# Layer 0's experts of a two-layer net: computed for every token, or by expert order with fetched rows and weights

## The chip, the cores and the metric

The kernel runs on one core of a Trainium2 chip (trn2). The metric is device time in microseconds (us) of one execution, smaller is better; three executions of the kernel before gave 1397.77, 1398.66 and 1400.67 us. Engines are named as the profile names them: PE (TensorE, matmuls; PEld is its weight load), DVE (VectorE), ACT (ScalarE), POOL (GpSimd), SP (SyncE, here only a DMA queue). DMA transfers are issued by SP, or by POOL where the rows to be fetched come from a table of indices.

## The reference, cut to what matters

The input is 2 sequences of 512 tokens, 256 wide: 1024 tokens. Two layers, each `x + s * silu(ffn)`, where `s` is attention and both parts read the same normalised rows:

```python
xn = _layernorm(x)
s = attn0(xn)                       # causal softmax attention, 16 heads of 16
g = silu(ffn0(xn)); x = x + s * g
xn = _layernorm(x)
s = attn1(xn)                       # gated delta rule, 16 key heads of 128, 32 value heads
g = silu(ffn1(xn)); x = x + s * g   # 2 shared and 16 routed experts, top 2

def ffn0(x, router_w, w1, w2, w3):  # 8 experts, 256 -> 128 -> 256
    logits = xf @ router_w.T
    topk_vals, topk_idx = jax.lax.top_k(logits, 2)
    topk_weights = softmax(topk_vals)
    gate = silu(einsum('nd,edf->enf', xf, w1))
    value = einsum('nd,edf->enf', xf, w2)
    expert_out = einsum('enf,efd->end', gate * value, w3)
    return sum over the two chosen of expert_out * topk_weights
```

The reference computes all 8 experts for every token and then selects two. Only 2048 of the 8192 (token, expert) pairs count.

## The kernel before, in words

Tokens lie in 8 tiles of 128 (n = 0 to 7; sequence b has tiles 4b to 4b+3). The program is one list. `Plan` holds pieces of work, each with parts on engines, a cost for each part and what it comes after. `Plan.arrange` (L128) repeatedly takes the ready piece that could start earliest by those costs, in steps of `GRAIN`, with ties decided by rank plus the engine's offset in the table `RANK`. What comes out is one order for each engine, which every engine then follows strictly, and the PSUM banks (8 of 128 x 2 KB) of each piece. So a piece that waits holds up all that stands behind it on its engine. The costs only make the order.

Layer 0 in the order of its work:

- The prologue loads inputs (among them the expert weights w1, w2, w3, 3 MB), normalises, makes Q, K, V. Q and K are written to DRAM and read back by 24 DMAs of 256 KB in another layout (`stack`).
- `rt`, `tp`: router logits, the two best of 8, their softmax, and by `gates` a table `gate` of 8 weights a token (six of them zero).
- Experts, dense: 16 blocks (expert e, sequence b). `exg` and `exv` are together 4 matmuls of 512 columns (L977), the two `exd` pieces 4 of 256 (L985). The profile counts each fp32 matmul of the code twice, so a block is 8 of L977 and 8 of L985 there. ACT takes silu (L1857), DVE the product (L1509) and the weighted sum into `facc` (L1521, L1523).
- Softmax: 64 pieces `p1` (scores on PE L995 and L1000, row maxima on DVE L1531), 32 for each sequence. When 32 are done `tn` (L1008, L1549) turns the maxima, SP writes them out and reads them back (`max`), and from then on the 16 steps of that sequence run: `sc` scores (L1016), exp on ACT (L1872), causal mask on POOL (L2097), `pv` (L1026). After each four steps `ov` (L1037) and a DVE reciprocal (L1555) and POOL product `am` (L2102).
- `op` (L1045): the output projection, on DVE `+bo` (L1560), times silu(experts) (L1562), plus x (L1564). `nrm`, `nr2`: the second layernorm. `ln1`: transposes into XH and XL.

Layer 1 begins with `gt` (router and gates, L930, at b = 0 and 1), convolution pieces `ck`, `cq`, `cv` (PE L930, DVE L1644: three operations a tile), up projections, then a chain of 64 units (`M` L1715 is its first DVE piece; L930 at 342.84 us stands in it), in whose gaps the remaining work is put. Layer 1's routed experts already work on rows in expert order: `cnt` counts and `places` computes tables (DVE L1405 to L1458), `slot` turns them to row numbers; for each group of 4 tiles of 128 rows `sr` fetches token rows (POOL L2135), `sw` weight rows (POOL L2151), `sT` transposes (PE L1169), `su` is the up product (PE L1178), `sd` down; `ss` (SP) writes the result rows, and `cb` fetches, for each token, its two result rows (POOL).

Of the kernel before, what the change touches and what calls it, by code (L numbers as in the profile page):

```python
# [30 lines left out]
GROUPS = (TILES + 3) // 4  # L31


def constants():
# [21 lines left out]


# [17 lines left out]
    "fWK": {"POOL": -59.896, "SP": -107.701}, "fWO": {"POOL": -20.631, "SP": 61.337},
    "fWV": {"POOL": 38.893, "SP": -91.558}, "fin": {"DVE": 5.828, "SP": -47.444}, "fs": {"ACT": 9.746},
    "fup": {"POOL": 27.276, "SP": -11.99}, "g0": {"ACT": -40.647}, "gg": {"DVE": -120.429, "PE": -10.129},
    "gram": {"DVE": 32.752, "PE": -0.939}, "gt": {"ACT": -141.264, "PE": -153.565},
    "kn": {"ACT": -7.778, "PE": -1.885, "POOL": -40.681}, "kns": {"ACT": 1.445},
    "ln1": {"ACT": -114.142, "DVE": -74.072, "PE": -25.594}, "max": {"SP": -146.911}, "mk": {"POOL": -21.707},  # L80
# [2220 lines left out]
```

## Time and profile before

| | us |
|---|---|
| median of 3 | 1398.66 (1397.77 to 1400.67) |
| profiled execution, its own time | 1398.75 |
| its span on the core | 1397.0 |
| PE busy | 1332.1 (95%) |
| DVE busy | 1127.7 (81%) |
| ACT busy | 950.0 (68%) |
| POOL busy | 698.5 (50%) |

The profile page gives busy time by engine, and in "slices" the share of 40 equal stretches. From the third slice on, PE is at 8 or 9 tenths to the end. The chain that ended last is 63% PE, 20% DVE, 6% ACT. The granted TensorE clock (PEclk, 1.0 is 2.4 GHz) is at 7 to 9 tenths in parts of the first seven slices and 9 later. Of the chain 4% is PE L977 and 2% PE L985, the dense experts. DMA is nearly full in the first two and a half slices (loads and the `stack` reads) and at some 2 tenths afterwards.

### The profile page before, as it was taken

What the parts mean: (1) busy time and instruction counts of PE and PEld (TensorE: products, weight loads), DVE (VectorE), ACT (ScalarE), POOL (GpSimd) and SP (SyncE); (2) the same over time, 40 slices, a digit from 0 to 9 for tenths busy, and PEclk for the clock granted to TensorE, in tenths of its full rate; (3) what the DMA queues carried; (4) which work ended last, traced back from release to release, by engine and by line L of the source; (5) the groups of instructions that cost most, each with busy time, mean ns of one, the idle gap of its engine ahead of it and who ended that gap; (6) DMA issues with size and microseconds to landing.
All of it is one profiled execution on the core that took longest, in us unless ns stands there. A gap on an engine that the chain in (4) does not pass through costs nothing.

```text
span 1397.0 us, 32580 instructions
## 1 busy us (share of the span) xinstructions
PE 1332.1 (95%) x12308; PEld 1089.2 (78%) x12308; DVE 1127.7 (81%) x2294; ACT 950.0 (68%) x2607; POOL 698.5 (50%) x806
## 2 busy tenths in 40 slices
PE   6999999788999999999999999999999998999997
PEld 3544446566888888888988898989888987889896
DVE  4487436889978788879798879797978888979886
ACT  3105752376777768787878787777777776787784
POOL 8012222328745475474655555656646558546431
PEclk9979999889999999999999999999999999999999
DMA  9950001212211121121311311312212114111000
GB/s 323 125 76 1 4 1 45 76 34 70 49 28 31 35 89 34 37 83 41 82 42 32 88 36 38 86 31 80 49 26 80 32 44 113 37 27 32 24 2 31
DMA packets 59507, 76.68 MB, mean 55 GB/s; under 512 B 6200, under 2 KB 46776, under 8 KB 59352
## 3 DMA queue, kind: packets, MB, share of 16 engines
q1 hardware_dynamic: 54616, 60.31, 17.9%
q0 software_dynamic: 4736, 14.29, 3.7%
q8 instruction: 98, 1.61, 0.5%
q14 instruction: 57, 0.47, 0.1%
HBM read 62.92 MB, written 11.67 MB: 53 GB/s over the span
## 4 chain that ended last, share of the span: by engine, by line
PE 63%; DVE 20%; ACT 6%; issue 4%; DMA 3%; POOL 3%; SPq 0%; POOLq 0%; DVEq 0%; ACTq 0%
PE ps L930 11%; PE ps L1313 6%; DVE yv L1644 4%; PE ps L977 4%; PE ps L1266 3%; DMA RC<-crow 3%; PE ps L1295 3%; PE ps L1282 2%; DVE yk L1644 2%; PE ps L1228 2%; PE ps L1218 2%; PE ps L1231 2%; PE ps L1267 2%; PE ps L985 2%; PE ps L1291 2%
## 5 line engine op out<-in xcount | busy, mean ns | idle before, releaser
L1988 ACT ACTIVATE XY<-ps 128x512 f16<-128x512 f32 x384 | 221.2, 599 | 71.4 <-PE ps L1231 70.2
L1734 DVE TENSOR_TENSOR ZL<-ps,cst 128x256 f16<-128x256 f32 x384 | 154.8, 418 | 34.7 <-PE ps L1218 34.0
L1644 DVE SCALAR_TENSOR_TENSOR yv<-ps,cw,yv 128x511 f32<-128x511 f32 (+2 forms) x192 | 143.4, 747 | 7.0 <-ACT yv L1925 2.3
L930 PE MATMUL ps<-XH,WVh 128*128 128x256 f32 (+1 forms) x384 | 133.4, 347 | 1.3 <-ACT hT L1973 1.3
L1313 PE MATMUL ps<-WO,OGT 128*128 128x256 f32 x512 | 126.3, 390 | 2.4 <-DVE OGT L1806 2.2
L930 PE MATMUL ps<-XH,WVl 128*128 128x256 f32 (+1 forms) x384 | 123.0, 320 | 0.0
L930 PE MATMUL ps<-XL,WVh 128*128 128x256 f32 (+1 forms) x384 | 122.8, 320 | 0.0
L2181 POOL TENSOR_TENSOR RC<-RC,dec 128x512 f32<-128x512 f32 x64 | 69.2, 1081 | 99.1 <-DMA RC<-crow 99.0
L1228 PE MATMUL ps<-ZL,XY 128*128 128x64 f16 x1536 | 105.5, 193 | 4.1 <-DVE ZL L1734 3.2
L2021 ACT ACTIVATE sq<-O 128x128 bf16<-128x128 f32 x256 | 79.8, 312 | 38.5 <-DVE O L1793 16.1
L1231 PE MATMUL ps<-XY,ZL 128*128 128x64 f16 x1536 | 105.0, 193 | 0.0
L1218 PEld LDWEIGHTS ps<-XY,LT 128*128 128x128 f16 x1536 | 80.2, 98 | 31.6 <-issue 12.4
L1218 PE MATMUL ps<-XY,LT 128*128 128x64 f16 x1536 | 100.5, 193 | 3.8 <-ACT XY L1988 2.4
L1313 PEld LDWEIGHTS ps<-WO,OGT 128*128 128x128 f32 x512 | 92.8, 191 | 13.5 <-issue 1.6
L1228 PEld LDWEIGHTS ps<-ZL,XY 128*128 128x128 f16 x1536 | 78.7, 97 | 29.1 <-issue 13.5
L2027 ACT ACTIVATE O<-O,small 128x128 f32<-128x128 f32 x256 | 82.7, 411 | 12.5 <-POOL small L2212 12.4
L1295 PEld LDWEIGHTS ps<-De,PT 128*128 128x128 f32 x512 | 74.4, 191 | 8.1 <-ACT De L2012 1.8
L1295 PE MATMUL ps<-De,PT 128*128 128x128 f32 x512 | 78.3, 278 | 1.7 <-ACT De L2012 1.6
L930 PEld LDWEIGHTS ps<-XH,WVl 128*128 128x128 f32 x384 | 72.5, 189 | 5.7
L2202 POOL TENSOR_TENSOR XY<-LT,cst 128x512 f16<-128x512 f16 x64 | 74.8, 1169 | 4.0 <-DVE W L1755 1.1
L930 PEld LDWEIGHTS ps<-XH,WVh 128*128 128x128 f32 x384 | 72.7, 189 | 4.7 <-ACT hT L1973 1.5
L2210 POOL TENSOR_SCALAR small<-small 128x4 f32<-128x4 f32 x64 | 12.5, 195 | 126.2 <-ACT sq L2021 123.8
(305 smaller groups left out, 4126.6 us busy)
## 6 DMA issues: line engine op xcount, KB each, us to landing
RC<-crow SPq DMA_DIRECT2D x128, 128.0 KB, 4.0
WV<-in_WV SPq DMA_DIRECT2D x16, 512.0 KB, 3.6
WK<-in_WK SPq DMA_DIRECT2D x16, 256.0 KB, 2.8
WO<-in_WO SPq DMA_DIRECT2D x16, 256.0 KB, 2.7
rows_out<-st SPq DMA_DIRECT2D x7, 512.0 KB, 4.3
KS<-spread SPq DMA_DIRECT2D x12, 256.0 KB, 19.3
QS<-spread SPq DMA_DIRECT2D x12, 256.0 KB, 26.8
w<-in_w SPq DMA_DIRECT2D x4, 512.0 KB, 8.6
```

The lines of the kernel that those rows point to most:

```text
L930: m = pe.matmul(o, a, b, start=c + k == 0, stop=c == 1 and k == 2)
L1218: m = pe.matmul(ps[:, bk, 64 * l:64 * l + 64], LT[:, u % 3, l, :], half(xy(u, 0)[:, l, :], k, 0), start=True, stop=True)
L1228: pe.matmul(ps[:, bk, 64 * l:64 * l + 64], y, half(z, k, 0), start=True, stop=True)
L1231: m = pe.matmul(ps[:, bk, 256 + 64 * l:320 + 64 * l], z, half(y, k, 1), start=True, stop=True)
L1295: m = pe.matmul(ps[:, bk, 256 + 128 * v:384 + 128 * v], PT[:, u % 4, 2 * b + v, :], De[:, b, v, :], start=True, stop=True)
L1313: m = pe.matmul(ps[:, bk, 256 * b:256 * b + 256], OGT[:, 2 * b + v, :], WO[:, h % 2, v, :], start=v == 0, stop=v == 1)
L1644: m = dve.scalar_tensor_tensor(out=dst[:, k:512], in0=ps[:, bk, 0:512 - k], scalar=cw[:, h, j, 3 - k:4 - k], in1=dst[:, k:512], op0=ALU.mu ...
L1734: leave(dve.tensor_tensor(half(ZL[:, k - 2], k, 0), p, lv(k), ALU.mult), "a", u, k)
L1988: leave(act.activation(changed(u, k), ps[:, bank("b", u, k), :].rearrange("p (c n t) -> p c n t", c=2, t=1 << (k - 1)), ACT.Copy), "b", u, k)
L2021: act.activation(sq[:, 1, :], O[:, u % 2, l, :], ACT.Square, accum_out=so[:, u % 2, l:l + 1]).then_inc(s_sqo, 1)
L2027: m = act.activation(O[:, u % 2, l, :], O[:, u % 2, l, :], ACT.Copy, scale=ro[:, u % 2, l:l + 1])
L2202: pool.tensor_tensor(xy(u, 1), LT[:, u % 3], spread4(cst[:, C_Y1:C_Y1 + 128]), ALU.mult).then_inc(s_y1, 1)
```

## The change

The dense experts of layer 0 are replaced by routed ones, of the same design as layer 1's. 1024 tokens with 2 experts each are 2048 rows; sorted by expert and padded to 128 for each of 8 experts they fill at most 16 + 7 = 23 tiles, in 6 groups of four (the last has three).

```diff
+TILES0 = 2 * 1024 // 128 + 7
+GROUPS0 = (TILES0 + 3) // 4
...
-    for k in range(16):
-        e, b = divmod(k, 2)
-        rank = -100 + 2 * k
-        old = [(("exd", *divmod(k - 3, 2), q), "PE") for q in range(2)] if k > 2 else []
-        x, y = ("exg", e, b), ("exv", e, b)
...
+    P.add(("xr0",), -400, ("SP", 1.0))
+    P.add(("cnt0",), -500, ("PE", 3.5, (("tp", 2), "DVE")), ("DVE", 9.0), takes=True, gives=("cnt0",))
+    P.add(("slot0",), -500, ("PE", 1.2, (("cnt0",), "DVE")), ("DVE", 0.2), takes=True, gives=("slot0",))
+    for g in range(GROUPS0):
+        rank = -400 + 6 * g
+        tiles = range(4 * g, 4 * g + tiles_of(g, TILES0))
+        old = [(("sd0", g - 2, q), "PE") for q in range(2)] if g > 1 else []
+        for t in tiles:
+            P.add(("sw0", t), rank, ("POOL", 1.0, (("cnt0",), "DVE"), (("sd0", g - 2, t % 4 // 2), "PE") if g > 1 else (("xr0",), "SP")), ("DMA", 1.9))
+            P.add(("sr0", t), rank, ("POOL", 1.0, (("slot0",), "DVE"), (("sT0", g - 1), "PE") if g else None), ("DMA", 0.8))
+        P.add(("sT0", g), rank, ("PE", 0.88, *[(("sr0", t), "DMA") for t in tiles]),
+              ("ACT", 0.91, (("sv0", g - 1), "PE") if g else None), takes=2, gives=("sT0", g))
+        P.add(("sg0", g), rank + 1, ("PE", 1.85, (("sT0", g), "ACT"), *[(("sw0", t), "DMA") for t in tiles]),
+              ("ACT", 0.62, *old), takes=True, gives=("sg0", g))
+        P.add(("sv0", g), rank + 2, ("PE", 1.85, (("sg0", g), "PE")), ("DVE", 0.6, (("sg0", g), "ACT")), takes=True, gives=("sv0", g))
         for q in range(2):
+            P.add(("sd0", g, q), rank + 3, ("PE", 0.92, (("sv0", g), "DVE")), ("DVE", 0.6, (("ss0", g - 1), "DMA") if g else None), takes=True, gives=("sd0", g, q))
+        P.add(("ss0", g), rank + 3, ("SP", 0.4, (("sd0", g, 0), "DVE"), (("sd0", g, 1), "DVE")), ("DMA", 2.6))
+    for n in range(NT):
+        P.add(("cb0", n), -400 + n, ("POOL", 2.2, (("ss0", GROUPS0 - 1), "DMA"), (("cb0", n - 4), "DVE") if n > 3 else None),
+              ("DMA", 0.8), ("DVE", 0.8))
     for b in range(2):
-        P.add(("g0", b), -60, ("ACT", 1.7, *[(("exd", 7, b, q), "DVE") for q in range(2)], (("g0", 0), "ACT") if b else None))
+        P.add(("g0", b), -200, ("ACT", 1.7, *[(("cb0", n), "DVE") for n in range(4 * b, 4 * b + 4)]))
...
+                elif x[0] == "sr0":
...
+                    pool.indirect_dma_start(rows0[:, k, :], None, xn0d, bass.IndirectOffsetOnAxis(ap=toki[:, t:t + 1], axis=0)
+                                            ).then_inc(d_in0[k], 16)
+                elif x[0] == "sw0":
...
+                    pool.indirect_dma_start(weights0[g % 2][k], None, A["ud0"],
+                                            bass.IndirectOffsetOnAxis(ap=rowi[:, t:t + 1], axis=0)).then_inc(d_wt0[g % 2][k], 16)
+                elif x[0] == "cb0":
+                    n = x[1]
+                    w.wait_ge(d_res0, 16 * GROUPS0)
...
+                    for k in range(2):
+                        pool.indirect_dma_start(wt0[:, n % 4, 256 * k:256 * k + 256], None, rows_out0,
+                                                bass.IndirectOffsetOnAxis(ap=posi[:, k, n:n + 1], axis=0)).then_inc(d_cb0[n % 4], 16)
```

`xr0` writes the normalised rows to DRAM (1 MB, `xn0d`). `cnt0`, `slot0` and `places` make the tables (`rowi`: weight rows of a tile; `toki`: token of each row; `posi`: where each token's two results lie). A group then takes 8 gathers on POOL (`sw0` 384 KB each, `sr0` 128 KB each), 8 transposes and an ACT copy (`sT0`), 8 matmuls of 128 columns for each of `sg0` and `sv0`, 4 of 256 for `sd0`, two DVE copies and one write of 512 KB (`ss0`). The weights have two sets of four buffers, the rows one: `sr0` of a group waits for the transposes of the group before. After the last group's write has landed, `cb0` makes 16 gathers, two for each n, and two DVE operations each; `g0` (silu) and `om` need them. The weights w1, w2, w3 are no longer loaded in the prologue; the host hands them over as one table `ud0` of rows of 3 KB.

Further parts: `op` is split. `op` (PE and DVE `+bo`) is free of the experts, `om` holds the two DVE operations that need them. `ln1` no longer comes after all expert matmuls. All of `RANK` has other numbers, for instance

```diff
-    "p1": {"DVE": 26.78, "PE": -1.261}, "pl": {"POOL": -95.917}, "pre": {"ACT": -110.761, "DVE": -90.125},
+    "p1": {"DVE": 25.623, "PE": -1.244}, "pl": {"POOL": -69.883}, "pre": {"ACT": -134.502, "DVE": -91.138},
-    GRAIN = 0.09700
+    GRAIN = 0.03900
-    DELAY = {"PE": 0.22, "DVE": 0.18, "ACT": 0.24, "POOL": 0.19, "SP": 0.1, "DMA": 0.1}
+    DELAY = {"PE": 0.22, "DVE": 0.18, "ACT": 0.24, "POOL": 0.19, "SP": 0.1, "DMA": 2.0}
```

and in layer 1 the planned DMA cost of `sr`, `sw`, `cb` is 0.8 in place of 2.5, and the write `ss` counts 0.4 on SP and 2.6 as DMA in place of 4.5 on SP. So the order of layer 1 changes too.

What stands on POOL around the begin of the softmax. The names: L2068 and L2070 split layer 1's first weights, L2097 is the mask, L2102 is `am`; before:

```order
L2068 CAST WKh<-WK 128x512
L2070 TENSOR_TENSOR WKl<-WK,WKh 128x512
L2068 CAST wabh<-wab 128x160
L2070 TENSOR_TENSOR wabl<-wab,wabh 128x160
L2097 AFFINE_SELECT PT<-PT 128x4x128 x8
L2102 TENSOR_TENSOR aT<-OT,rB 128x512
```

In the changed kernel the same place (L2127 is the split, L2202 `sw0`, L2190 `sr0`, L2154 the mask):

```order
L2127 TENSOR_TENSOR wabl<-wab,wabh 128x160
L2202 DMA wt<-in_ud,rowi 128x768 x4
L2190 DMA rows<-xn0d,toki 128x256 x4
L2202 DMA st<-in_ud,rowi 128x768 x2
L2202 DMA wt<-in_ud,rowi 128x768 x2
L2190 DMA rows<-xn0d,toki 128x256 x4
L2202 DMA wt<-in_ud,rowi 128x768 x4
L2190 DMA rows<-xn0d,toki 128x256 x4
```

So the first gathers stand behind the split of the weights, and the gathers of groups 0 to 3 ahead of the first mask. Further down POOL has the write-backs' gathers `cb0` (L2213) between two groups of masks, 13 masks ahead of them:

```order
L2154 AFFINE_SELECT PT<-PT 128x4x128 x3
L2159 TENSOR_TENSOR aT<-OT,rB 128x512
L2154 AFFINE_SELECT PT<-PT 128x4x128 x3
L2213 DMA wt<-rows_out,posi 128x256 x16
L2154 AFFINE_SELECT PT<-PT 128x4x128 x3
```

All 16 gathers stand together; the 14th to 32nd masks are behind them.

On PE, the rows ahead of the turned maxima of sequence 0 (L1008 before). Before, dense expert matmuls stand between the `p1` pieces:

```order
L985 MATMUL ps<-w,hT 128x256 x4
L995 MATMUL ps<-KS,QS 128x128 x2
L1000 MATMUL ps<-cb 128x128 x2
L995 MATMUL ps<-KS,QS 128x256 x2
L1000 MATMUL ps<-cb 128x128 x2
L977 MATMUL ps<-xnT,w 128x512 x2
```

In the changed kernel (L1041 and L1046 are `p1`, L1013 `sT0` of group 1, L1023 `sg0` and `sv0`, L1054 `tn`):

```order
L1013 MATMUL ps<-cst,rows 128x128 x8
L1041 MATMUL ps<-KS,QS 128x384 x2
L1046 MATMUL ps<-cb 128x128 x2
L1041 MATMUL ps<-KS,QS 128x512 x2
L1046 MATMUL ps<-cb 128x128 x2
L1041 MATMUL ps<-KS,QS 128x128 x2
L1046 MATMUL ps<-cb 128x128 x2
L1023 MATMUL ps<-XS,st 128x128 x4
L1023 MATMUL ps<-XS,wt 128x128 x4
L1041 MATMUL ps<-KS,QS 128x256 x2
L1046 MATMUL ps<-cb 128x128 x2
L1054 MATMUL ps<-cst,Mp 32x128 x4
```

So `tn` of sequence 0 now stands behind `sT0`, `sg0` and `sv0` of group 1 (`sv0` repeats the two L1023 rows right ahead of L1054). In the changed kernel 42 `p1` pieces and the matmuls of two groups stand ahead of the first `sc`; before, 44 `p1` pieces 20 of the 64 matmuls of L977 and 12 of the 64 of L985. Ahead of the first `M` of layer 1, the changed order has more of layer 1's other PE work than before (K convolution 60 matmuls for 42, V 36 for 12, Z 36 for 24, up 12 for 24), and seven more convolution tiles on DVE.

## Rows read from the trace of the kernel before

**Rows 1.** Windows view: stretches of the span by engine, granted clock, DMA share.
```profile
core 0: us, PE busy (x) PEld busy (x) DVE busy (x) ACT busy (x) POOL busy (x), PEclk, DMA share, GB/s
65.00:104.00 39.00, 38.28 (x194) 19.19 (x192) 34.93 (x53) 1.88 (x2) 4.49 (x6) 0.74 0.63 83
104.00:212.00 108.00, 106.57 (x616) 49.00 (x614) 57.09 (x67) 66.11 (x89) 29.16 (x39) 1.00 0.01 2
212.00:258.00 46.00, 36.68 (x135) 23.66 (x134) 34.39 (x82) 8.61 (x18) 13.83 (x16) 0.92 0.17 55
258.00:320.00 62.00, 51.79 (x256) 42.93 (x257) 53.50 (x127) 40.10 (x85) 20.67 (x24) 0.86 0.18 52
320.00:1397.00 1077.00, 1044.79 (x10949) 925.15 (x10948) 920.51 (x1882) 816.09 (x2386) 601.77 (x710) 0.99 0.19 49
```

**Rows 2.** Chain that ended last, in time: start us, us, what; dense matmuls, `cnt`, layer 1.
```profile
228.14 1.73 PE ps L985 x8
229.87 3.43 PE ps L977 x8
296.61 3.41 PE ps L1153 x16
342.84 1.49 PE ps L930 x6
```

**Rows 3.** PE timeline (start us, us, engine, line, operation): routed group of layer 1.
```profile
490.29 1.56 PE L1178 MATMUL ps<-st,wt 128*128 128x128 f32 x12
```

**Rows 4.** POOL timeline around the end of the stack reads.
```profile
87.31 0.61 POOL L2068 CAST WKh<-WK 128x512 fp32r<-128x512 f32 x1 [57.99 <-DMA WK<-in_WK]
91.52 0.52 POOL L2070 TENSOR_TENSOR wabl<-wab,wabh 128x160 fp32r<-128x160 f32 x1
```

**Rows 5.** POOL timeline: two row gathers of layer 1, one after the other.
```profile
341.42 0.95 POOL L2135 DMA_INDIRECT st<-xnd,toki  x1 [0.30 <-issue]
342.67 0.95 POOL L2135 DMA_INDIRECT st<-xnd,toki  x1 [0.30 <-issue]
```

**Rows 6.** DMA issues of the whole span: KB each where known, median us to landing.
```profile
st<-xnd,toki POOLq DMA_INDIRECT x31, 3.6
wt<-in_ud,rowi POOLq DMA_INDIRECT x24, 4.5
rows_out<-st SPq DMA_DIRECT2D x7, 512.0 KB, 4.3
```

**Rows 7.** One line's landings (L2135, the row gathers), with their spread.
```profile
DMA to landing us min/median/max: 2.7/3.6/5.1
```

**Rows 8.** PE timeline: `tn` of sequence 0, then the first score.
```profile
97.07 0.60 PE L1008 MATMUL ps<-cst,Mp 128*32 128x128 f32 x4
104.02 0.51 PE L1016 MATMUL ps<-QS,KS 64*128 64x512 f32 x2
```

**Rows 9.** Windows view of one PE line each: L1016 (`sc`), then L1026 (`pv`).
```profile
104.00:212.50 108.50, 26.50 (x128) 11.94 (x128) 1.00 0.01 2
...
104.00:212.50 108.50, 23.86 (x256) 5.03 (x256) 1.00 0.01 2
```

**Rows 10.** PE timeline, end of layer 0: last `pv`, last `op`, first gates.
```profile
212.03 0.42 PE L1026 MATMUL ps<-PT,V 128*32 128x128 f32 x8
241.76 5.34 PE L1045 MATMUL ps<-wo,aT 128*128 128x256 f32 x24
258.29 0.69 PE L930 MATMUL ps<-XH,wabh 128*80 128x512 f32 x1 [3.75 <-DVE XL L1585]
```

**Rows 11.** Groups by shape, 0 to 330 us: busy us, mean ns, idle; the reciprocal.
```profile
L1555 DVE RECIPROCAL rB<-ps 128x512 f32<-128x512 f32 x8 | 26.9, 3358 | 11.0 <-PE ps L1037 11.0
```

**Rows 12.** DVE timeline: a convolution tile; layer 1's first `M`; an `op`.
```profile
264.54 2.31 DVE L1644 SCALAR_TENSOR_TENSOR yk<-ps,cw,yk 128x511 f32<-128x511 f32 x3
320.31 0.68 DVE L1715 TENSOR_TENSOR M<-ps,E 128x512 f32<-128x512 f32 x1
253.56 0.42 DVE L1560 TENSOR_TENSOR st<-ps,bo 128x256 f32<-128x256 f32 x1
```

More of the change, by code:

```diff
@@ L75 @@
[L75 to L80, printed above, removed]
@@ L91 @@
-    "su": {"ACT": -16.946, "PE": 8.309}, "sw": {"DMA": -100.52, "POOL": -124.214}, "sx": {"POOL": -65.71},
-    "tn": {"DVE": -40.39, "PE": -186.124}, "tn0": {"DVE": -59.954}, "top": {"ACT": -153.89, "DVE": -156.062},
[3 rows of a table removed]
[4 rows of a table added]
+    "cb": {"DMA": 53.563, "DVE": 100.046, "POOL": 124.422}, "cb0": {"DMA": -7.938, "DVE": 19.605, "POOL": 12.029},
+    "cc": {"POOL": 17.016}, "ck": {"ACT": -22.284, "DVE": 80.478, "PE": -3.081}, "cnt": {"DVE": 1.226, "PE": -22.434},
+    "cnt0": {"DVE": -18.804, "PE": -2.993}, "cq": {"ACT": -46.76, "DVE": 50.605, "PE": -1.71},
@@ L96 @@
+    "sv0": {"DVE": 45.357, "PE": 6.262}, "sw": {"DMA": -51.94, "POOL": -99.591}, "sw0": {"DMA": 6.433, "POOL": 1.813},
+    "sx": {"POOL": -65.71}, "tn": {"DVE": -93.687, "PE": -200.173}, "tn0": {"DVE": -40.719},
+    "top": {"ACT": -195.908, "DVE": -148.291}, "tp": {"ACT": 69.034, "DVE": -62.104},
[3 rows of a table added]
 }
@@ L987, in run_tensor @@
+                    signal(m, *x)
+                elif what == "sd0":
+                    g, q = x[1:]
+                    bk = enter(*x)
+                    w.wait_ge(*done("sv0", g))
+                    for k in range(2 * q, min(2 * q + 2, tiles_of(g, TILES0))):
+                        m = pe.matmul(ps[:, bk, 256 * (k % 2):256 * (k % 2) + 256], hT0[:, g % 2, 128 * k:128 * k + 128],
+                                      weights0[g % 2][k][:, 512:768], start=True, stop=True)
                     signal(m, *x)
@@ L1502, in run_vector @@
                     softmax_of_two()
-                    gates(0, 8, 7)
-                elif what == "exv":
-                    e, b = x[1:]
-                    h_ = hT0[:, (2 * e + b) % 3, :]
-                    w.wait_ge(*done("exg", e, b))
+                    choose(0, 8)
+                elif what == "cnt0":
+                    places(("cnt0",), 0, 8)
+                elif what == "slot0":
+                    w.wait_ge(*full("slot0"))
+                    leave(dve.tensor_copy(toki[:], ps[:, bank("slot0"), 0:32]), "slot0")
+                elif what == "sv0":
+                    n = 128 * tiles_of(x[1], TILES0)
+                    w.wait_ge(*done("sg0", x[1]))
@@ L1558, in run_vector @@
                     w.wait_ge(*full(*x))
+                    for q in range(2):
+                        w.wait_ge(*full("sd0", GROUPS0 - 1, q))
+                    leave(dve.tensor_tensor(st[:, n, :], ps[:, bank(*x), 0:D], bo[:], ALU.add), *x)
+                elif what == "om":
+                    n = x[1]
+                    w.wait_ge(*done("op", n))
                     w.wait_ge(s_g0, n + 1)
-                    leave(dve.tensor_tensor(st[:, n, :], ps[:, bank(*x), 0:D], bo[:], ALU.add), *x)
-                    w.wait_ge(*done(*x))
                     dve.tensor_tensor(st[:, n, :], facc[:, n, :], st[:, n, :], ALU.mult).then_inc(s_og, 1)
```

407 lines of the change are left out of this document (225 added, 182 removed), and 24 rows, old and new, of the table RANK.

## The prediction, made before the changed kernel ran

> **What bounds the kernel now.** I read the windows first: they show who is busy in each stage. In all of layer 1 from 320 us on, PE is busy 1044.8 of 1077 us; in the softmax stage 104 to 212 us it is 106.6 of 108, at full clock [rows 1]. So up to 247 us, the end of the last output projection [rows 10], PE work taken away would count in full if nothing else came in. From 258 to 320 us the table of the first row turns: DVE is busy 53.5 of 62 us and PE waits for it [rows 1]. The chain in time shows the dense experts as links of 3.43 us (eight matmuls of L977) and 1.73 us (eight of L985), one behind the other [rows 2]. Ahead of 104 us the POOL timeline and the PE timeline say why the softmax doesn't start sooner: layer 1's first weights land at 87.3 us behind the stack reads, the queue's end [rows 4], and `tn` stands at 97.07, the first score at 104.02 [rows 8].
>
> **PE work.** Removed: 16 blocks x (3.43 + 1.73) = 82.6 us [rows 2]. Added: layer 1's routed group shows 12 matmuls of 128 columns in 1.56 us, 0.13 each [rows 3]; the profile counts each of the code twice, so `sg0` and `sv0` are 16 each, 4.2 us; eight transposes of that width 1.0; `sd0` has the shape of a block's L985, 1.7. That is 6.9 us a group of four and 39.7 for 5.75 groups. `cnt0` and `slot0` are as in layer 1, where 16 matmuls of `cnt` took 3.41 us [rows 2]; there are twice as many with its other half, at most 6.8, and fp16 ones in `slot0`: between 4 and 9, I take 7. Net: 82.6 - 39.7 - 7 = 36 us less on PE. If PE stayed as full as it is, the kernel would take 1363.
>
> **What it adds: a chain of transfers.** Two gathers in a row start 1.25 us apart on POOL [rows 5] and land 3.6 us after issue [rows 6]; weight rows 4.5. On POOL, `sw0` and `sr0` stand behind the split of layer 1's weights, over at 92.0 [rows 4]; the tables they need are ready long before by my reading (the count runs while the stack is read), so the in-order queue is what makes them late, not their data. Four `sw0`, four `sr0`: the last is issued at 92.0 + 8 x 1.25 - 1.25 = 100.8 and lands at 104.4. Only then can `sT0` of group 0 run, and PE, in order, stands there with 22 of 64 `p1` done. Before, PE had 38.3 of 39 us filled here [rows 1]. Group 1's eight are issued by 110.8 and land at 114.4. Behind that on PE: transposes 1.0, copy on ACT 1, `sg0` 2.0, a `p1`, `sv0` 2.0, and with the clock at the level of 0.74 that rows 1 show here, some 1.2 us more: `tn` at 121.6 or later, in place of 97.07. From `tn` to the first score 6.95 us go by for the round trip of the maxima [rows 8]: 128.6. PE work that piles up at low clock could make it 134. I take **131, 27 us later**.
>
> **From the first score to the end of the projections.** Before: 104.0 to 247.1 (241.76 + 5.34), 143 us [rows 8, 10], some 2 of it idle. 44 of 64 of the 977 and 52 of 64 of the 985 matmuls lie in it: 54.9 x 44/64 + 27.7 x 52/64 = 60.2. So the rest is 81 us: softmax, `p1`, `op`. After: 131 + 81 + 1.5 (two more `p1`) + 3.75 groups x 6.9 = 25.9, makes 239 if PE never waits. It does, at two places.
>
> First, groups 2 to 5 wait for gathers again: `sr0` of a group stands behind transposes of the group before and behind masks, and each costs at least one landing, 3.6 us [rows 6], that softmax pieces cover in part. Between 0 (all covered) and 4 x 5.1 = 20 (the slowest landing of rows 7, none covered) I take 8.
>
> Second, the write back. `sd0` of group 5 stands on PE behind 13 further `p1`, 23 of 64 score pairs, 8 of 32 `pv`. The lines' windows give 26.5 / 64 = 0.41 us a pair and 23.9 / 32 = 0.75 a step [rows 9]; these overlap (the lines of 104 to 212 sum to 120 busy where PE has 106.6), so 0.89 of it: 8.5 + 5.3, `p1` at some 0.57 (estimate: one and a half pairs) 7.5, two `ov` 1.9, and 25.9: 131 + 49 + 8 = 188. Copy 0.7, issue 0.4, landing 4.3 [rows 6]: 193.5. Then all 16 `cb0` gathers stand in one piece on POOL, 16 x 1.25 = 20 us, to 213.5, with masks 14 to 32 behind them. PE has 5 steps of `pv`, some 9 pairs, 9 `p1` to fill from 188, about 13 us: idle from 201 or so until 214. That is the new wait, 12 us. Sum: 239 + 8 + 12 = 259, less 7 for sequence 1's projection, which now stands behind other work: **the last `pv` at about 252, before 212** [rows 10]. What stood behind the softmax before (26 us of dense blocks) stands ahead of it now.
>
> **Into layer 1.** `om` of sequence 0 needs `g0`, which needs `cb0`, ready by about 217: no wait. The gates of layer 1 begin at about 253.5 (258.3 before, [rows 10]); `ln1` no longer waits for experts. From there the path is DVE's: 62 us before, to the first `M` at 320.3 [rows 12], of which DVE idles 8.5 [rows 1]. New behind the gates: the last reciprocal 3.4 [rows 11]; `op`, `om` and the statistics of sequence 1, 12 operations of 0.42 [rows 12] and 1.8; seven more convolution tiles of 2.31 [rows 12], 16.2; one more Z pair 1.3. Sum 27.8, and 6.5 of the idle time takes some of it: 253.5 + 62 + 27.8 - 6.5 = 336.8, **16 us later** than before. But the PE work placed ahead of the first `M` is worth about 10 us (K 18, V 24, Z 12 matmuls more, up 12 fewer, 42 at 1.49 / 6 = 0.25 us each, [rows 2]), and PE is what layer 1 is bound by [rows 1]. So + 16 - 10 = **+6 us**. Against the profiled 1398.75 that is 1404.8; against the median 1398.66 the same within 0.1. The new orders of layer 1 (planned DMA costs) I price at 0, between -6 and +6: PE idles 32 of 1077 us there.
>
> **The prologue.** 3 MB of loads go. The spread writes start when Q and K are ready, and the stack reads run at 125 GB/s to 83 us whatever stood ahead [rows 1]: 0, at best 2 us.
>
> **A rule weighed.** Landings of row gathers lie between 2.7 and 5.1 us, with DVE busy 920.5 of 1077 us in layer 1 [rows 1, 7]. The Trainium skill (SBUF — State Buffer, "SBUF: two separate sides") says that a DMA issued by GpSimd can be starved of descriptors while DVE runs certain fp32 copies within SBUF. By that rule gathers of six groups would each take the slowest landing, 1.5 us more: +9 us in the first chain and later. The trace's spread is mild, so I leave the sum as it is. Another page (DMA: Bandwidth & Descriptors, "Anatomy of one DMA — SWDGE (gpsimd) path") gives 2.0 us plus bytes over 436 GB/s, an estimate of 2.3 us for 128 KB; the trace shows 3.6, and by the page the sum would be some 8 us smaller.
>
> **Rivals.**
> 1. *The waits overlap better* (25%): the landings of groups 2 to 5 are covered by softmax pieces, and PE has enough scores and `p1` to do while `cb0` is issued. Then the 8 and the 12 fall away: the last `pv` at 232, and DVE's tail is fed some 18 us earlier: 1404 - 18 = 1386. For it: softmax work between the groups. Against: exp may run only three steps ahead of `pv`.
> 2. *PE's saving comes through* (13%): as rival 1, and the tables let the gathers of group 0 hide behind `p1`: of 36 us, 8 are lost: 1398.75 - 28 = 1371. Against it: POOL isn't free before 92.0, and DVE holds the tail.
> 3. *Slower, the clock* (12%): PE stands still from 85 to 114 us and again near 201; the granted clock was 0.74 in 65 to 104 with PE full [rows 1]. If it stays at half (1.2 GHz) for 30 us behind each of the idle stretches, PE loses up to 15 us: 1404 + 15 = 1419. It is slower than before from a loss of 1 us on, since the forecast itself is.
> 4. *No net effect* (8%): DVE tail 16 and PE credit 16: 1399.
> The forecast has 42%.
>
> **The numbers.** What can be told from no change here is 0.2%, 2.8 us. The forecast's own range is 1397 to 1412, by -6 to +6 in layer 1 and the few us either way of the 8. Faster: .25 + .13, less .01 for a rival 1 that ends near 1396, .37. Same: rival 4's .08 and .09 of the forecast's .42, where it ends under 1401.5. Slower: the rest of it, .33, and .12, with .01 from rival 1's other end: .46. Range for 8 in 10: 1378 to 1424, which leaves out rival 2 and the end of rival 3.
>
> **What would show it.** In the windows PE's total down by some 36 us, PE idle between 85 and 104 and near 201 to 214. `tn` of sequence 0 at 120 to 127, first score near 131, the last `pv` near 252, first `M` near 337. On POOL 16 gathers take 20 us, and a mask behind them whose scores are long done. Wrong, if the first score comes before 120, or if PE is over 95% busy between 131 and 250, or if the first `M` comes before 325.

## The result: slower by 27 us, and the profile after

Four executions of the changed kernel gave 1424.18 to 1430.01 us, median 1427.02; the kernel before, beside it, 1399.66. The ratio is 1.0195, 95% interval 1.0167 to 1.0224. The forecast was slower, but 1404, with an upper end of 1424: the direction held, the size did not. The profiled execution took 1428.63 us with a span of 1426.9, 29.9 more than before.

The windows of the changed kernel, in the columns of [rows 1]:

```profile
46.00:65.00 19.00, 10.14 (x51) 8.76 (x50) 10.37 (x53) 0.21 (x1) 0.00 (x0) 0.53 1.07 126
65.00:104.00 39.00, 17.61 (x92) 8.30 (x92) 18.07 (x24) 0.00 (x0) 13.26 (x15) 0.50 0.87 163
104.00:212.00 108.00, 90.43 (x626) 60.03 (x626) 61.89 (x85) 48.22 (x62) 60.31 (x67) 0.88 0.47 140
212.00:258.00 46.00, 39.05 (x242) 16.92 (x242) 26.27 (x31) 28.45 (x44) 19.39 (x26) 0.86 0.03 7
258.00:320.00 62.00, 52.26 (x268) 40.47 (x269) 58.11 (x130) 32.40 (x79) 28.10 (x35) 0.97 0.24 77
320.00:1426.00 1106.00, 1056.20 (x10994) 934.70 (x10992) 924.25 (x1907) 820.33 (x2394) 606.08 (x714) 0.99 0.18 48
```

PE's total fell from 1332.1 to 1300.6 us, 31.5 less, near the 36 forecast. Its idle time rose from 64.9 to 126.3, by 61.4; the difference is the 29.9. In 46 to 65 us PE is busy 10.1 of 19 us (before, all 19.0), and in 65 to 104 us 17.6 of 39 where it was 38.3; its granted clock there is 0.50, the lower of its two levels. In 104 to 212 it idles 17.6 us, before 1.4.

The timelines of POOL, PE and DVE in the changed kernel show each link of the forecast chain (in brackets the idle time before the row, and what ended it):

```profile
87.65 0.61 POOL L2125 CAST WKh<-WK 128x512 fp32r<-128x512 f32 x1 [58.33 <-DMA WK<-in_WK]
92.55 1.22 POOL L2202 DMA_INDIRECT wt<-in_ud,rowi  x1 [0.19 <-issue]
101.57 0.95 POOL L2190 DMA_INDIRECT rows<-xn0d,toki  x1 [0.30 <-issue]
...
212.23 0.95 POOL L2213 DMA_INDIRECT wt<-rows_out,posi  x1 [0.30 <-issue]
213.18 1.88 POOL L2154 TENSOR_SCALAR_AFFINE_SELECT PT<-PT 128x512 f32<-128x512 f32 x3
```

```profile
104.41 1.94 PE L1013 MATMUL ps<-cst,rows 128*128 128x128 f32 x8 [20.79 <-DMA rows<-xn0d,toki]
125.40 0.60 PE L1054 MATMUL ps<-cst,Mp 128*32 128x128 f32 x4
137.53 0.79 PE L1062 MATMUL ps<-QS,KS 64*128 64x512 f32 x2 [5.25 <-DMA QS<-rowmax]
213.89 1.51 PE L1072 MATMUL ps<-PT,V 128*32 128x384 f32 x8 [7.64 <-POOL PT L2154]
262.20 0.44 PE L965 MATMUL ps<-XH,wabh 128*80 128x512 f32 x1 [0.39 <-DVE XL L1635]
341.02 0.79 PE L1247 MATMUL ps<-KT 128*128 128x128 f32 x2 [10.97 <-ACT KN L1999]
```

```profile
335.87 2.72 DVE L1501 SCALAR_TENSOR_TENSOR O<-cst,small 128x2048 f16<-128x2048 f32 x1
338.51 0.41 DVE L1684 TENSOR_TENSOR dec<-dec 128x256 f32<-128x256 f32 x1
338.85 0.28 DVE L1685 TENSOR_SCALAR dec<-dec 128x256 f32<-128x256 f32 x1
339.05 0.68 DVE L1765 TENSOR_TENSOR M<-ps,E 128x512 f32<-128x512 f32 x1
```

PE stands 20.8 us for the first group's rows; `tn` is at 125.4 (before 97.07, [rows 8]), the first score at 137.5 (104.02, [rows 8]); 16 result gathers end at 213.18 and the 14th mask comes right behind them, with PE waiting 7.6 us for it. The gates begin at 262.2 (258.29, [rows 10]), the first `M` at 339.05, 18.7 us later than in [rows 12]. Ahead of it DVE works without a gap, the tables of layer 1 (L1501 is their last large step) last, while PE waits 11 us.

Behind the first `M` the two kernels part further. All 64 `M` pieces of each, by line (min/median/max ns, first and last start), before and after:

```profile
L1715 DVE TENSOR_TENSOR M<-ps,E x64: 680/684/692, 320.3 to 1342.7; 128x512 f32<-128x512 f32 x64
```

```profile
L1765 DVE TENSOR_TENSOR M<-ps,E x64: 677/684/693, 339.1 to 1367.1; 128x512 f32<-128x512 f32 x64
```

From first to last `M`: 1022.4 before, 1028.0 after. From the last `M` to the end of the span: 54.3 before, 59.8 after. So 29.9 = 18.7 + 5.6 + 5.5, but for rounding. The forecast was +16.5 at the first `M` and 10 us *less* behind it.

### The profile page after: what moved, and what is told of

It reads as the page before. It is cut to its first block and busy times, and to the rows that moved or that the text cites. A ratio compares the mean times of both kernels' runs of the same rounds, so it can differ in the third digit from the quotient of the medians.

```text
span 1426.9 us, 32743 instructions
## 1 busy us (share of the span) xinstructions
PE 1300.6 (91%) x12376; PEld 1088.2 (76%) x12376; DVE 1117.4 (78%) x2267; ACT 941.0 (66%) x2599; POOL 755.7 (53%) x868
## 5 line engine op out<-in xcount | busy, mean ns | idle before, releaser
L1784 DVE TENSOR_TENSOR ZL<-ps,cst 128x256 f16<-128x256 f32 x384 | 154.2, 418 | 31.5 <-PE ps L1268 30.5
L965 PE MATMUL ps<-XH,WVh 128*128 128x256 f32 (+1 forms) x384 | 133.6, 348 | 3.2 <-DVE QC L1694 1.7
L965 PE MATMUL ps<-XH,WVl 128*128 128x256 f32 (+1 forms) x384 | 123.0, 320 | 0.0
L965 PE MATMUL ps<-XL,WVh 128*128 128x256 f32 (+1 forms) x384 | 123.0, 320 | 0.0
L1278 PEld LDWEIGHTS ps<-ZL,XY 128*128 128x128 f16 x1536 | 81.8, 98 | 33.5 <-issue 13.6
L2078 ACT ACTIVATE sq<-O 128x128 bf16<-128x128 f32 x256 | 79.4, 310 | 42.0 <-DVE O L1843 17.0
L1268 PEld LDWEIGHTS ps<-XY,LT 128*128 128x128 f16 x1536 | 77.1, 98 | 24.4 <-issue 13.2
L1577 DVE TENSOR_REDUCE Mp<-ps 128x2 f32<-128x256 f32 (+1 forms) x64 | 50.4, 816 | 43.8 <-PE ps L1046 43.0
L2283 POOL CAST MHi<-M 128x512 f16<-128x512 f32 x64 | 39.1, 612 | 77.8 <-DVE M L1765 77.8
L965 PEld LDWEIGHTS ps<-XH,WVh 128*128 128x128 f32 x384 | 72.9, 190 | 7.6 <-DVE QC L1694 1.9
```

The lines of the kernel that those rows point to most:

```text
L965: m = pe.matmul(o, a, b, start=c + k == 0, stop=c == 1 and k == 2)
L1268: m = pe.matmul(ps[:, bk, 64 * l:64 * l + 64], LT[:, u % 3, l, :], half(xy(u, 0)[:, l, :], k, 0), start=True, stop=True)
L1278: pe.matmul(ps[:, bk, 64 * l:64 * l + 64], y, half(z, k, 0), start=True, stop=True)
L1784: leave(dve.tensor_tensor(half(ZL[:, k - 2], k, 0), p, lv(k), ALU.mult), "a", u, k)
L2078: act.activation(sq[:, 1, :], O[:, u % 2, l, :], ACT.Square, accum_out=so[:, u % 2, l:l + 1]).then_inc(s_sqo, 1)
```

## The experiments

Fourteen further runs were made, in four jobs; in each job the kernel before ran too, and the last column has its median. The places in this table are read from the timeline of each profiled execution, in us; "behind" is from last `M` to the end of the span.

| kernel | first score | last pv | first M | last M | behind | median (range) | before, same job |
|---|---|---|---|---|---|---|---|
| before | 104.0 | 212.2 | 320.3 | 1342.7 | 54.3 | | |
| changed | 137.5 | 259.7 | 339.1 | 1367.1 | 59.8 | 1427.0 (1424.2-1430.0) | 1399.7 |
| e1 | 105.4 | 251.8 | 351.6 | 1376.2 | 65.9 | 1441.9 (1438.5-1443.8) | 1397.4 |
| e2 | 121.3 | 245.4 | 339.8 | 1371.6 | 55.6 | 1444.3 (1429.0-1446.5) | 1397.4 |
| e3 | 114.7 | 239.0 | 319.6 | 1346.5 | 60.5 | 1412.2 (1408.7-1415.7) | 1397.4 |
| e5 | 144.6 | 266.8 | 346.2 | 1372.9 | 58.2 | 1433.0 (1428.6-1434.1) | 1397.4 |
| e4 | 135.2 | 257.0 | 338.3 | 1373.1 | 58.5 | 1429.4 (1419.4-1433.3) | 1397.4 |
| e5b | 130.7 | 252.8 | 332.9 | 1357.6 | 59.5 | 1422.4 (1418.9-1425.6) | 1397.4 |
| e6 | 120.5 | 241.0 | 332.8 | 1354.7 | 57.4 | 1413.2 (1410.9-1413.8) | 1397.4 |
| e8 | 128.3 | 252.5 | 333.1 | 1356.4 | 59.8 | 1420.8 (1418.0-1426.8) | 1397.4 |
| changed again | 131.9 | 251.5 | 332.0 | 1358.0 | 59.8 | 1421.5 (1419.5-1425.8) | 1398.8 |
| e10 | 117.5 | 236.1 | 316.2 | 1341.2 | 59.7 | 1405.1 (1402.6-1409.7) | 1398.8 |
| e11 | 113.5 | 237.7 | 318.2 | 1342.1 | 58.2 | 1403.5 (1402.0-1407.3) | 1398.8 |
| e12 | 115.4 | 233.7 | 308.4 | 1361.7 | 57.3 | 1419.8 (1417.3-1423.2) | 1398.8 |
| e13 | 117.9 | 241.7 | 323.5 | 1353.8 | 57.6 | 1412.1 (1406.8-1413.5) | 1399.0 |
| e14 | 103.7 | 211.9 | 320.0 | 1344.2 | 60.4 | 1406.2 (1404.6-1406.9) | 1399.0 |

### Whose loss is it: the order numbers or the routed experts (e1, e2)

e1 is the kernel before with the changed kernel's numbers and planned DMA costs; e2 the changed kernel with the old `RANK` entries and `GRAIN`.

```diff
 # e1, in the kernel before                 # e2, in the changed kernel
-RANK = {... as before}                    -RANK = {... as changed}
+RANK = {... as changed}                   +RANK = {... as before; sr0, sw0, ... as changed}
-    GRAIN = 0.09700                       -    GRAIN = 0.03900
+    GRAIN = 0.03900                       +    GRAIN = 0.09700
```

> The kernel before with the changed kernel's order numbers (RANK, GRAIN, DELAY, planned DMA costs of layer 1), dense experts kept. Theory A (the loss behind the first M, 11 us, comes from the new order of layer 1): 1406 to 1412, with first M near 320 as before and some 11 us more from there to the end. Theory B (it comes from what the routed layer 0 leaves behind, an idle and slow PE at 330 to 360 us, the new order itself costs nothing): 1396 to 1402.

> The changed kernel with the numbers of before for every piece that both have (RANK and GRAIN); the routed pieces keep theirs. Theory A (new numbers cost 11 us behind the first M): 1416. Theory B (they cost nothing): 1424 to 1430. In both the first score stays near 137 us and the last of the 16 result gathers near 213, since the weights' split and the gathers keep their order on POOL.

Neither theory foresaw this: e1 is 3.1% slower than before (interval 1.0290 to 1.0326), e2 3.4% (1.0323 to 1.0358). In e1 most of it is there at the first `M` (351.6 for 320.3), so a swap of all numbers doesn't isolate the stretch behind it. What can be taken from both is the last stretch: 65.9 us with the new numbers, 55.6 with the old ones. The profiled execution of e2 was its fastest of five, and its spread is 17 us (below, the reads).

### The gathers' place on POOL (e3) and the loads' place on SP (e10)

e3 moves the write of the rows ahead on SP and plans the split of layer 1's weights behind the gathers of groups 0 and 1:

```diff
+            w.wait_ge(s_xn[0], NT)
+            sp.dma_start(xn0d.rearrange("(n p) d -> p n d", p=128), st[:]).then_inc(d_xr0, 16)
             for t in (2, 3, 0, 1):
...
-        P.add(("fWK", h), -100, ("POOL", 1.9))
+        P.add(("fWK", h), -100, ("POOL", 1.9, (("sr0", 7), "POOL")))
```

> The changed kernel with the rows' write to DRAM issued ahead of the spread writes, and the gathers of groups 0 and 1 ahead of the split of layer 1's weights on POOL. Theory gather chain (POOL's order makes the first groups late): the first gather starts near 67 us instead of 92.5, the first transposes no later than 90 instead of 104.4, the first score 15 to 20 us earlier (118 to 122), the kernel 10 to 18 us faster than the changed one: 1409 to 1417. Rival (the gathers compete with the stack reads for DMA, so what they gain the stack loses): the stack's end moves from 83 to 90 or later, the first score is not over 8 us earlier, 1420 to 1427.

The gain was 15 us against the changed kernel's 1427.0 and 9 against its second run's 1421.5, both from other jobs. The first score came at 114.7, even earlier than expected, and the first `M` at 319.6, no later than before.

e10 leaves every engine's order alone but SP's: the loads for layer 1 and the rows' write are issued ahead of the stack reads.

```diff
             fetch(WK, "WK", 1, d_WK)
+            w.wait_ge(s_xn[0], NT)
+            sp.dma_start(xn0d.rearrange("(n p) d -> p n d", p=128), st[:]).then_inc(d_xr0, 16)
             for b in range(2):          # the 24 stack reads, up to here ahead of these loads
...
```

> The changed kernel, orders of all engines but SP's untouched: on SP the rows' write and the loads of layer 1's first weights are issued ahead of the 24 stack reads instead of behind. Theory queue (the gathers are late because POOL waits for these loads): the split is over before 60 us, the first gather starts when its table is there, 60 to 62 us, the first transposes follow the 22 p1 at 84 to 88 with no wait, the first score 15 to 20 us earlier (118 to 122), total 1406 to 1414, spread between executions 4 us or less. Rival (stack reads pay for it): first score 125 or later, 1416 to 1424.

> The changed kernel unaltered, on the chip of the next three. In eight traces the split of layer 1's weights on POOL, which waits for the end of the stack reads, began anywhere from 75.6 to 88.4 us. Theory reads (this end varies from execution to execution, and the changed kernel follows it since the gathers stand behind the split): tn of sequence 0 comes 37 to 39 us after the split's begin, as at 87.65 and 125.4, and at 82.54 and 120.6; total 1418 to 1430. Rival (the variation is of the chip and shows in the kernel before too): before varies as much, by 5 us or more.

POOL's timeline in e10:

```profile
37.97 0.61 POOL L2126 CAST WKh<-WK 128x512 fp32r<-128x512 f32 x1 [8.65 <-DMA WK<-in_WK]
60.52 1.71 POOL L2203 DMA_INDIRECT wt<-in_ud,rowi  x1 [17.82 <-DVE small L1484]
```

And PE's:

```profile
87.73 1.94 PE L1014 MATMUL ps<-cst,rows 128*128 128x128 f32 x8 [0.62 <-DMA rows<-xn0d,toki]
```

The split is done by 43 us and the gathers begin as soon as DVE has their table; PE waits 0.6 us for them instead of 20.8. e10 takes 1405.1 where the changed kernel, on the same chip, takes 1421.5: **16 us of its loss was SP's order**, the split's loads and the write of the rows behind the 24 stack reads, shown by an edit that changes nothing but their place.

Two links were moved at once, in e3 as in e10: POOL's split waits for the loads of WK, and the row gathers need the rows' write. In the changed kernel this write stands behind those loads (SP's timeline, then the view of this line):

```profile
74.33 2.63 SPq L883 DMA_DIRECT2D xn0d<-st  x1
...
DMA to landing us min/median/max: 16.6/16.6/16.6
```

It landed at 90.9 us, and the first row gather was issued at 97.83. So had only the split not stood in the way, the row gathers could have begun 6.9 us earlier at most, by this trace; the rest of what e10 won needs the earlier write as well. No run moved one link alone. The stack did pay something: the first `p1` waited until 67.2 us (60.8 in the changed kernel's second run). In both e3 and e10 the first `M` comes 1 to 4 us *before* that of the kernel before, so the DVE tail is not a fixed 16 us but hangs on when the softmax ends: the first `M` comes 80.6 and 80.1 us behind the last `pv`, in the changed kernel's two runs 79.4 and 80.5. The remaining 6 us (1.0061, 1.0039 to 1.0084) lie behind the first `M`: in the profiled execution of e10, its fastest, 8.0 us are lost there and 4.1 won ahead of it.

The second run of the changed kernel has a median 5.5 us under the first, with the first score at 131.9, the 131 of the forecast. The split began at 86.9 there, at 82.54 in e8, at 75.6 in e2. `tn` followed it by 37.1 us in this run, 37.8 in the first and 38.1 in e8. So the changed kernel follows the landing of these loads, behind the end of the reads. That this landing makes the spread of its total isn't shown: the kernel before spans 5 us too in its 7 executions of that job (1396.5 to 1401.4), and e10, which waits for no late load, was expected to spread 4 us or less and spread 7.1.

### PE at half clock behind its wait (e5, e5b)

The clock didn't fall because of this wait: it stood at 0.53 in 46 to 65 us and 0.50 in 65 to 104 already (windows above), and in e10 it is 0.50 in 76 to 84 us with PE busy all 8 of them. The question is when it rises. Both add matmuls with discarded results ahead of group 0's transposes, 36 and 20:

```diff
                 elif what == "sT0":
                     g = x[1]
                     bk = enter(*x)
+                    for _ in range(20 if g == 0 else 0):
+                        pe.matmul(ps[:, bk, :], ident, cst[:, 0:512], start=True, stop=True)
```

> The changed kernel with 36 further matmuls of 512 columns (their results are thrown away) on PE ahead of the first group's transposes, where PE stands idle from 83 to 104 us at half clock. Theory clock (the slow clock behind the idle stretch costs time): transposes and p1 pieces from 104 to 112 run at full clock, 3 to 4 us won at the first score (134), 1423 to 1425 in all. Rival (what follows waits for the gathers anyway): no change, 1426 to 1428; also if the added matmuls don't raise the clock and last past 104, 2 to 10 us slower.

> As the kernel with 36 added matmuls, which took 33 us of PE at half clock and so ended 12 us after the rows had landed: now 20 of them, 18.6 us by that run, ending near 102, ahead of the landing at 104.4. Theory clock: the stretch from 104 to 112 runs at full clock, first score 3 us earlier than 137.5, total 1423 to 1426. Rival (the clock rises only with full work behind it and stays at half while only these run; the wait on the gathers stays): 1426 to 1429.

e5 was mis-sized: 36 matmuls of fp32 took 33.4 us and held the transposes until 116.8. e5b's windows, then the changed kernel's in its second run:

```profile
83.00:104.00 21.00, 19.32 (x48) 8.50 (x47) 0.59 (x1) 0.00 (x0) 14.35 (x17) 0.94 0.62 192
104.00:112.00 8.00, 8.00 (x61) 6.46 (x60) 4.79 (x7) 2.90 (x3) 5.57 (x6) 1.00 0.69 225
```

```profile
83.00:104.00 21.00, 0.32 (x3) 0.33 (x3) 0.73 (x2) 0.00 (x0) 13.93 (x16) 0.50 0.65 190
104.00:112.00 8.00, 8.00 (x47) 6.51 (x46) 2.61 (x3) 2.90 (x3) 5.97 (x7) 0.65 0.73 236
```

With work in the gap the clock is 0.94 to 1.00 (2.4 GHz), without it 0.50 (1.2 GHz) until some 8 us after the wait, and PE does 61 matmuls in 8 us instead of 47. `tn` came 34.7 us behind the split's begin (120.83 after 86.17) instead of 37.1 to 38.1: the clock costs about 3 us up to `tn`. At the first score nothing of it is left against the second run (44.5 us behind the split's begin against 45.0). In the total it can't be told: 1422.4 against 1427.0 and 1421.5.

### The maxima's round trip (e8, e11)

```diff
                 elif x[0] == "sw0":
...
+                    if g == 3:
+                        w.wait_ge(d_maxq[0], 32)
```

> The changed kernel with the weight gathers of group 3 held back until the row maxima of sequence 0 are read back. Theory contention (write and read of the maxima take 12.1 us from tn to the first score instead of 6.95 because gathers fill the DMA engines, 0.7 to 0.9 busy): first score at 134 to 135 instead of 137.5, total 1424 to 1428. Rival (the gathers in flight are those of group 2, issued before, so holding group 3 changes nothing there and only delays group 3): first score 137, total 1428 to 1433.

> As e10_loads_first, and the weight gathers of group 3 held back until the maxima of sequence 0 are read. Theory contention: tn to first score 8 to 9 us instead of 10 or more in e10, total 1 to 3 us under e10. Rival (the PE work behind hides it, and group 3 gets later): within 1 us of e10 or up to 3 slower.

SP's queue in the changed kernel, then in the kernel before:

```profile
126.97 0.34 SPq L866 DMA_DIRECT2D rowmax<-MT  x1
130.37 0.58 SPq L870 DMA_DIRECT2D QS<-rowmax  x2
```

```profile
98.42 0.34 SPq L840 DMA_DIRECT2D rowmax<-MT  x1
100.06 0.59 SPq L844 DMA_DIRECT2D QS<-rowmax  x2
```

The write of 64 KB took 3.4 us from issue to the next in the changed kernel, 1.6 before, and `tn` to first score 12.1 instead of 6.95, with the DMA engines 0.72 busy in 126 to 137 us by the window. Held back, in e8 it is 7.7 (120.6 to 128.3). Against the first run that supports contention, but the second run of the unaltered kernel has 7.9 without the edit. So the round trip is 1 to 5 us longer than before, by execution, and that the gathers in flight are the cause isn't shown. e11 is e10 with this edit: 7.5, where e10, expected at 10 or more, has 7.7, so there was nothing to take away. e11 is 1.6 us under e10, inside their ranges.

### The 16 result gathers in one piece (e4)

```diff
-(("cb0", n - 4), "DVE") if n > 3 else None),
+(("cb0", n - 4), "DVE") if n > 3 else None, (("mk", *STEPS[11 + n]), "POOL")),
...
                 elif what == "kn":        # ACT, with the order changed it has to wait for POOL
+                    w.wait_ge(s_aT, 8)
```

> The changed kernel with each pair of result gathers (cb0 n) planned behind mask number 11 + n, so that they stand on POOL among the masks, not as one piece of 16. Theory wait on masks (PE idles 7.6 us for mask 14 and is slow behind it, clock 0.52 to 0.70 from 200 to 230 us): last pv 8 to 12 us earlier than 259.7, first M 4 to 8 us earlier than 339.1, total 1419 to 1424. Rival (DVE's work in a row sets the first M, whenever the softmax ends; with the results later, g0 and om come later): last pv earlier, but first M within 3 us of 339, total 1425 to 1431.

Against the changed kernel's first run the last `pv` moved by 3 us only, the first `M` by 1, the median not at all (1429.4). Counted from the split's begin, e4's last `pv` is at 168.6 us, between the second run's 164.6 and the first's 172.1. The numbers fall as the rival said: PE waits 0.5 us for the 14th mask instead of 7.6, the last result gather is issued at 227.6 instead of 212.2, and the total gains nothing. But the edit is no clean cut. It goes through `arrange`, and other orders moved with it: behind the softmax POOL has a split of WV ahead of the last `am`, and DVE's pieces stand in another order. That the wait by itself is worth next to nothing is likely, not shown.

### Layer 1's tables ahead of the first M (e12)

```diff
-P.add(("cnt",), -3.5, ("PE", 3.5, (("top", 2), "DVE")),
+P.add(("cnt",), -3.5, ("PE", 3.5, (("top", 2), "DVE"), (("pt", 0), "DVE")),
```

> As e10_loads_first, and layer 1's count and its tables (11.7 us of DVE in a row, ahead of the first M, while PE idles 11 us) planned behind the DVE pieces of unit 0. Theory DVE tail (the first M waits for DVE's work in a row, this piece above all): first M 9 to 12 us earlier than in e10, total 5 to 10 us under e10, near the 1397 of before. Rival (the tables then hold unit 0's and unit 1's DVE pieces, so the chain loses behind the first M what it gained): first M earlier, total within 3 us of e10.

The first `M` came 7.8 us earlier than in e10, and the kernel was 14.7 us slower: from first to last `M` it takes 1053.3 us instead of 1025.0. The tables now stand between the second and the third `M` (315.35 to 328.3 us), and PE waits 8.2 us there for one of unit 0's DVE pieces behind them; in 340 to 380 us PE is busy 32.6 of 40 at a clock of 0.83. Both theories missed: it was neither faster nor within 3 us of e10. An early first `M` is no gain by itself.

### The numbers of layer 1 behind the first M (e6, e13, e14)

e6 is e3 with the old offsets for all of layer 1. e13 is e11 and e14 the kernel before, each with the other's offsets for late pieces alone:

```diff
+    late = (k in UNITS and n >= 8 or k in HEADS and n >= 3 or k in ("sw", "sr") and n >= 4
+            or k in ("sT", "su", "sd", "ss") and n >= 1 or k in ("cb", "xb", "fs", "fin"))
+    return LATE if late else RANK
...
-                                              rank + RANK.get(label[0], {}).get(eng, 0.0)
+                                              rank + rank_table(label).get(label[0], {}).get(eng, 0.0)
```

> The kernel with early gathers, and the offsets of before for all pieces of layer 1 (those of layer 0 and GRAIN stay as changed). Theory order (the retuned numbers lengthen the stretch from the last M to the end, 60 us with them in three kernels, 54 to 56 with the old ones in two): last M to end 54 to 57, total 1405 to 1409. Rival (that stretch follows from how layer 1 begins, and numbers fitted to one timeline are bad in another, as both mixed kernels were at 1442 and 1444): 1415 to 1445.

> The kernel before, and the same late pieces of layer 1 planned with the offsets of the changed kernel. Theory order numbers: first M unchanged at 320, last M to end 58 to 62, total 1402 to 1408. Rival (the new numbers cost nothing by themselves): 1396 to 1400, last M to end 54 to 55.

> As e11_loads_first_calm, and the late pieces of layer 1 (units from 8, heads from 3, routed groups from 1, the end) planned with the offsets of before. Theory order numbers (last M to end is 59.7 us in all kernels with the new numbers, 54.3 to 57.4 with the old ones): last M to end 54 to 57, first M unchanged near 316, total 1396 to 1401, no slower than before. Rival (numbers fit a timeline, and a mixture is worse than either): 1403 to 1415.

e14's `M` pieces:

```profile
L1823 DVE TENSOR_TENSOR M<-ps,E x64: 675/682/692, 320.0 to 1344.2; 128x512 f32<-128x512 f32 x64
```

First `M` as before, first to last 1024.2 (1.8 more), then 60.4 (6.1 more); the median is 7.2 us over the kernel before, ratio 1.0052, interval 1.0038 to 1.0065. So **the new numbers for late pieces cost the dense kernel 7 us**, most of it in the last stretch. What that stretch holds, by windows from the last `M` on, before and changed:

```profile
1342.70:1397.00 54.30, 45.58 (x442) 40.04 (x440) 37.50 (x90) 33.16 (x108) 9.51 (x14) 0.94 0.06 21
```

```profile
1367.10:1426.90 59.80, 50.12 (x498) 44.33 (x496) 41.15 (x98) 36.70 (x124) 12.18 (x17) 0.96 0.06 19
```

4.5 us more PE work, 56 matmuls, is still to be done behind the last `M`: other work went ahead of the units' in the gaps. The opposite swap failed. e6 has 1021.9 and 57.4 where e3 has 1026.9 and 60.5, 8 us better behind the first `M`, and a first `M` 13 us later. e13 was expected at 1396 to 1401 and took 1412.1, 8.6 us more than e11, as the rival had it: its first `M` is 5 us later and it takes 1030.3 us to the last. Its split of the pieces at unit 8 leaves nothing of the gain. That the numbers cost the changed kernel 5 to 8 us too is argued, not shown. For it speaks the last stretch: 57.3 to 60.5 us in the ten runs with the routed experts and the new numbers, 55.6 to 57.6 in the three with old ones (e2, e6, e13). But the two groups overlap, since e12 kept the numbers and has 57.3, and no version gave the loss back in the total.

The stretch between first and last `M` has a second cause. Its first 50 us, before, changed, and e10:

```profile
320.30:370.00 49.70, 45.77 (x497) 38.73 (x495) 47.36 (x91) 33.61 (x85) 39.75 (x46) 0.98 0.31 75
```

```profile
339.10:388.80 49.70, 43.08 (x430) 36.08 (x431) 36.85 (x72) 32.62 (x74) 39.19 (x45) 0.88 0.25 74
```

```profile
316.20:366.00 49.80, 42.36 (x444) 35.67 (x445) 38.70 (x75) 33.14 (x75) 40.95 (x48) 0.95 0.28 75
```

Seven of the profiled executions have the changed kernel's PE order but for the added matmuls. In the two whose clock is 0.88 here (changed, e5) the stretch takes 1028.0 and 1026.7 us; in the five at 0.94 or 0.95 (e5b, e8, changed again, e10, e11) 1023.3 to 1026.0. So of the 5.6 us that the first run lost between first and last `M`, e14's numbers answer for 1.8, and some 3 go with the slow clock of its opening, by that comparison; why it differs by execution is open.

## Why the prediction was right or wrong

- *What goes and comes on PE*: forecast 36 us less; measured 31.5, with part of the rest at half clock. Right.
- *The first gathers*: forecast last issue 100.8, landing 104.4; measured 101.57 and the transposes at 104.41. Right in time. The reason given, POOL's queue and "not their data", is half of it: the rows themselves were in DRAM only at 90.9, since their write stood behind the same reads, and e10 moved both.
- *`tn`, first score*: forecast 121.6 or later and 131; measured 125.4 and 137.5, in the second run 124.0 and 131.9. The mechanism is right; left out was that the round trip of the maxima could take longer than the 6.95 us of before: 12.1 and 7.9 us, with the cause not shown. The clock was taken too mildly: I carried over 0.74 from before, but it was 0.50, with PE busy 17.6 of 39 us.
- *Result gathers*: forecast 193.5 to 213.5; measured 193.21 to 213.18. The wait of PE there: forecast 12, measured 7.6 for the mask. It is in the trace as forecast. e4, which takes it away and moves other orders too, gains nothing, so its price in the total was probably too high.
- *Last `pv`*: forecast 252; measured 259.7, in the second run 251.5. *Gates*: forecast 253.5, measured 262.2 and 254.1.
- *First `M`*: forecast 336.8, +16.5; measured 339.05, +18.7, and 332.0 in the second run. The closeness is in part luck: the gates came 8.7 us later than forecast, and the stretch behind them took 76.9 us (77.9 in the second run), not 83.3. DVE is busy 72.9 us in it, 19.1 more than the 53.8 of before, where I had added 27.8. Also, I had it as a DVE sum that would stand whatever came ahead; e10 moves it to 316.2 by 16 us of earlier start.
- *PE credit of 10 us behind it*: **this step failed**, and with it the size of the forecast; in its place stands a loss of 11.2 us. "The PE work placed ahead of the first `M` is worth about 10 us" was counted in the order up to the first matmuls of the chain (L1247), not up to the first `M`, and it left out what moved the other way. All L930 (L965) matmuls from the first `M` on, by window, before and changed:

```profile
320.30:1397.00 1076.70, 296.50 (x1445) 216.15 (x1443) 0.99 0.19 49
```

```profile
339.10:1427.00 1087.90, 292.82 (x1416) 213.75 (x1416) 0.99 0.18 48
```

29 matmuls and 3.7 us less, not 42 and 10; and eight of an expert's down product and the 16 of `slot` came to stand behind the first `M`, some 2.6 us. In sum PE has 1046.8 us of work behind it (996.7 + 50.1), before 1044.5 (998.9 + 45.6). So 2.3 of the 11.2 us are more work and 8.9 more idle time (41.0 us for 32.2). For that idle time the forecast had only the new orders of layer 1, which I had put at 0, "between -6 and +6". What the runs show for it is 7 us by e14, in the dense kernel, and some 3 us for the slow opening; how the changed kernel's own loss divides stays open.
- *Sum*: 16.5 - 10 became 18.7 + 11.2. Of the 23 us between forecast and measured in the profiled executions, 21 are of the second term.
- *Rivals*: the faster ones fell on the idle time in 65 to 104 and 200 to 213 us. Rival 3 (the clock, 1419) was right in that PE ran at half clock; but of the distance to 1427 it explains about 3 us at the first place, by e5b, and some 3 of the 11.2 behind the first `M`; most of it is the failed term.
- *A page weighed*: the rule of the Trainium skill (SBUF — State Buffer, "SBUF: two separate sides"), by which DVE copies can starve gathers issued by GpSimd, would have shown as issues of more than 1.25 us. In the changed kernel the gathers of groups 0 and 1 keep 1.25 us but for the first, with DVE mostly idle. In e10 two issues took 1.71 and 2.69 us, while DVE built the tables from SBUF to SBUF; the longer one stands beside its longest step (POOL, then DVE):

```profile
63.80 2.69 POOL L2203 DMA_INDIRECT wt<-in_ud,rowi  x1 [0.30 <-issue]
```

```profile
63.38 2.28 DVE L1502 SCALAR_TENSOR_TENSOR rows<-cst,small 128x2048 f16<-128x2048 f32 x1
```

Gaps of 1.2 to 1.5 us lay between later ones, beside the `p1` maxima, which DVE reads from PSUM. The first part fits the rule's direction, but the DMA engines were full with the stack reads at the same time (their share is 1.07 in 60 to 68 us), and no run here tells the two apart.

No version beat the kernel before. The best, e11, is 0.5% slower (1.0048, 1.0030 to 1.0066): 5 us, where the numbers' 7 us would be enough to explain it. Whether numbers found anew for e11's timeline would bring it under 1399 was not tried.
